# Two transformer layers with routed experts on one core: layer-norm chains of the attention moved to GpSimd and taken earlier, quantising moved off GpSimd, early shared sums added later

## What is computed

```python
x = x + quantised_product(layernorm(x), ctx)     # activations and ctx rounded to e4m3 in blocks of 128
x = x + moe(layernorm(x), 32 experts, top 4, plus a shared expert)
x = x + attention(layernorm(x), k=ctx, v=ctx)    # 8 heads of 32, 256 positions
x = x + moe(layernorm(x), 8 experts, top 2, plus a shared expert in two halves)
```

## Time and profile before

| | |
|---|---|
| median of 3 runs | 466.25 us (465.55 to 466.74) |
| the profiled execution | 468.48 us, of which the span of its instructions is 466.4 us |
| mean granted TensorE clock | 0.908 of full |
| busy share of the span | PE 76%, DVE 60%, ACT 43%, POOL 35% |

### The profile page before, as it was taken

One profiled execution on the slowest core, in us unless ns is written; L12 is line 12 of the kernel. 1 busy time (PEld: TensorE's weight loads), 2 busy tenths in 40 slices (PEclk: granted clock), 3 DMA queues, 4 the chain that ended last, 5 costly groups with the idle time before them and its releaser, 6 DMA issues.

```text
span 466.4 us, 8276 instructions
## 1 busy us (share of the span) xinstructions
PE 356.5 (76%) x2359; PEld 203.0 (44%) x2359; DVE 280.5 (60%) x791; ACT 201.7 (43%) x467; POOL 164.5 (35%) x220
## 2 busy tenths in 40 slices
PE   0003397789999999999983665667766899998996
PEld 0002184435555545555442444444554345444664
DVE  3999859645555555555558639395877155554365
ACT  1301245255555555555413737355731355554221
POOL 2060204756666666666310000002310533300560
PEclk9999998999999999999995558596985699999999
DMA  8999970094222322345557930000002223321232
GB/s 236 353 302 271 341 192 0 23 298 128 91 91 91 91 92 92 92 106 172 164 183 296 272 107 3 0 1 0 4 3 88 69 91 92 94 68 45 80 114 79
DMA packets 28780, 57.32 MB, mean 123 GB/s; under 512 B 3825, under 2 KB 13937, under 8 KB 28737
## 3 DMA queue, kind: packets, MB, share of 16 engines
q1 hardware_dynamic: 20785, 38.38, 27.0%
q0 software_dynamic: 6336, 17.31, 12.7%
q10 hardware_dynamic: 1616, 1.11, 0.8%
HBM read 44.72 MB, written 12.06 MB: 122 GB/s over the span
## 4 chain that ended last, share of the span: by engine, by line
PE 66%; DVE 18%; issue 8%; ACT 3%; POOL 2%; DMA 2%; DVEq 0%; ACTq 0%; SPq 0%; POOLq 0%
PE bank L1226 19%; PE bank L1253 13%; PE bank L1100 5%; PE bank L1237 5%; PE bank L1302 4%; PE bank L1217 3%; PE bank L1111 3%; PE bank L1314 3%; PE bank L1151 2%; PE bank L1089 2%; DMA x_sb<-x 2%; DVE x_sb L947 1%; DVE att_nm L979 1%; PE bank L1333 1%; DVE st L704 1%
## 5 line engine op out<-in xcount | busy, mean ns | idle before, releaser
L1226 PE MATMUL bank<-arena,xT 128*64 x272 | 112.5, 496 | 1.3 <-ACT xT L608 1.3
L1229 PE MATMUL bank<-xn,xT 128*64 128x384 f32 (+1 forms) x272 | 112.5, 497 | 0.0
L482 POOL DMA_INDIRECT xg<-m_xn,tab x68 | 65.7, 967 | 61.3 <-PE bank L1217 52.5
L1253 PE MATMUL bank<-arena,hT 96*64 (+1 forms) x272 | 70.4, 381 | 1.9 <-DVE hT L906 1.3
L1256 PE MATMUL bank<-xn,hT 96*64 96x256 f32 (+1 forms) x272 | 70.4, 381 | 0.0
L601 ACT ACTIVATE xn<-arena 128x768 f32 (+1 forms) x68 | 56.3, 827 | 21.9 <-issue 21.8
L931 DVE TENSOR_TENSOR hh<-sg,bank 128x192 f32<-128x192 f32 (+1 forms) x71 | 24.8, 350 | 63.0 <-ACT sg L624 63.0
L474 POOL DMA_INDIRECT m_ys<-ysb,dest x48 | 47.4, 988 | 23.9 <-issue 12.8
L1253 PEld LDWEIGHTS bank<-arena,hT 96*64 96x64 f32 (+1 forms) x272 | 34.8, 135 | 38.7 <-issue 28.2
L608 ACT ACTIVATE xT<-bank 128x256 f32<-128x256 f32 x71 | 27.2, 383 | 47.8 <-PE bank L1217 47.1
L1302 PE MATMUL bank<-arena,xn 32*128 32x256 f32 x128 | 23.0, 521 | 27.7 <-issue 21.4
(11 more groups left out here) (173 smaller groups left out, 615.2 us busy)
## 6 DMA issues: line engine op xcount, KB each, us to landing
arena<-w_gu SPq DMA_DIRECT2D x3, 3456.0 KB, 18.8
arena<-w_dn SPq DMA_DIRECT2D x3, 1728.0 KB, 24.5
arena<-m_ys SPq DMA_DIRECT2D x8, 512.0 KB, 5.5
m_ys<-ysb SPq DMA_DIRECT2D x20, 128.0 KB, 1.7
arena<-w_gu SPq DMA_DIRECT2D x2, 1056.0 KB
m_xn<-xn SPq DMA_DIRECT2D x2, 1024.0 KB, 6.4
arena<-w_gu SPq DMA_DIRECT2D x1, 1408.0 KB
arena<-w_gu SPq DMA_DIRECT2D x1, 1152.0 KB, 11.5
```

The source lines that it names most:

```text
L482: nc.gpsimd.indirect_dma_start(out=xg[:, b, :], out_offset=None, in_=xn_d[L.name], in_offset=bass.IndirectOffsetOnAxis(ap=d["tab"][:, s:s ...
L1226: T.matmul(bank[2 + s % 2][0:BLOCK, 0:2 * J2], xT[:, s % 2, c, 0:BLOCK], arena[:, bass.ds(off + c * 2 * J2, 2 * J2)], start=(c == 0), stop ...
L1229: return T.matmul(bank[2 + s % 2][BLOCK:P, 0:2 * J2], xT[:, s % 2, c, BLOCK:P], gu2[:, s % 2, cols], start=(c == 0), stop=(c == C - 1), ti ...
L1253: T.matmul(bank[6 + s % 2][0:BLOCK, 0:H], hT[0:L.J, s % 2, a, 0:BLOCK], arena[0:L.J, bass.ds(off + L.gu + a * H, H)], start=(a == 0), stop ...
```

## The change

- **Quantising.** The two GpSimd operations on ctx go to DVE: the addition right after the factors, the subtraction (to `wq`) between the two halves. The scaling of the normalised tokens leaves DVE for ACT, as 16 copies of 128 columns with a factor per token, in place; DVE waits for 8 of them before each half. The two three-operand forms on `amx` and `rin_x` become plain `tensor_scalar`. The semaphore `c_mag` is gone, `rin_ready` and `xs_ready` are new.
- **Early shared sums.** `early_shared` on GpSimd only multiplies. The additions to x stand in the loop of `gathers`, each ahead of the gather that waits for the same buffer's `t_done`. A result keeps its own buffer of `ysb` until then, so ACT no longer waits for the additions, and DVE no longer waits for all of them before the pair tiles; it waits for one of them before it writes that buffer.
- **Attention.** One table `chains` holds six chains: after which head the statistics are given, the tiles, whether they are for attention (then scaled, and normalised by ACT), and the head at which the result is used. GpSimd computes all six, with the negated means. Tiles 0 and 1 are one chain on DVE. Tiles 0 to 3 are taken before the first head, 4 to 7 at heads 1, 2, 6 and 7.

```diff
+        chains = [(-1, (2, 3), True, 2), (2, (4, 5), True, 7), (7, (6, 7), True, 12),
+                  (11, (0, 1), False, 15), (19, (2, 3), False, 23), (27, (4, 5), False, 31)]
...
-            pool.wait_ge(c_mag, 1)
-            link(nc.gpsimd.tensor_tensor(v_c, v_c, c_c, ALU.add))
-            nc.gpsimd.tensor_tensor(wq.rearrange("p b k n -> p (b k n)"), v_c, c_c, ALU.subtract).then_inc(wq_ready, 1)
...
+            def early_add(L, n):
+                q, t = M[L.name]["early"], early_work[L.name][n][1]
+                pool.wait_ge(q["y_copied"], n + 1)
+                nc.gpsimd.tensor_tensor(x_sb[:, t, :], x_sb[:, t, :], ysb[:, n, :], ALU.add).then_inc(q["added"], 1)
...
                     if s >= BUFS:
                         pool.wait_ge(m["t_done"], s - BUFS + 1)
+
+                        if s - BUFS < n_early[L.name]:
+                            early_add(L, s - BUFS)
...
             def deviations(i):
+                _, tiles, asked, _ = chains[i]
+                a, b = tiles[0], tiles[-1] + 1
                 pool.wait_ge(stats_ready, i + 2)
-                inverse_deviation(nc.gpsimd, link, by_pool[sorted(by_pool)[i]], 1.0)
-                pool.sem_inc(rstd_ready, 1)
+                inverse_deviation(nc.gpsimd, link, tiles, SCALE if asked else 1.0)
+                link(nc.gpsimd.tensor_tensor(nmr[:, a:b], mv[:, a:b, 0], rstd[:, a:b], ALU.mult))
+                nc.gpsimd.tensor_scalar(nmr[:, a:b], nmr[:, a:b], -1.0, None, ALU.mult).then_inc(rstd_ready, 1)
...
+            act.wait_ge(rin_ready, 1)
+            for a in range(16):
+                block_of = v_x[:, a * P:(a + 1) * P]
+                nc.scalar.activation(block_of, block_of, ACT.Copy, scale=rin_x[:, a:a + 1]).then_inc(xs_ready, 1)
...
-                if g in by_pair:
-                    queries(3 + sorted(by_pair).index(g), by_pair[g])
+                for i, (_, tiles_of, asked, turn) in enumerate(chains):
+                    if asked and turn == g:
+                        act.wait_ge(rstd_ready, i + 1)
+                        for t in tiles_of:
+                            normalise(t, q_ready)
...
-            link(V.scalar_tensor_tensor(out=amx[:], in0=amx[:], scalar=ACT_EPS, in1=amx[:], op0=ALU.max, op1=ALU.max))
+            link(V.tensor_scalar(amx[:], amx[:], ACT_EPS, None, ALU.max))
             link(V.reciprocal(rin_x[:], amx[:]))
-            link(V.scalar_tensor_tensor(out=rin_x[:], in0=rin_x[:], scalar=FP8_MAX, in1=rin_x[:], op0=ALU.mult, op1=ALU.max))
...
+            V.tensor_scalar(rin_x[:], rin_x[:], FP8_MAX, None, ALU.mult).then_inc(rin_ready, 1)
+
+            link(V.tensor_tensor(v_c, v_c, c_c, ALU.add))
...
+                dve.wait_ge(xs_ready, 8 * (i + 1))
...
+                if i == 0:
+                    V.tensor_tensor(wq.rearrange("p b k n -> p (b k n)"), v_c, c_c, ALU.subtract).then_inc(wq_ready, 1)
...
+            queries([0, 1])
+            take(2)
+            take(3)
+            statistics(chains[0][1]).then_inc(stats_ready, 1)
+            for g in range(4):
+                head_max(g)
+
+            takes = {1: 4, 2: 5, 6: 6, 7: 7}
```

More of the change, by code:

```diff
@@ L291, in mk_xattn_ffn @@
         n_early = {"m0": 4, "m1": 1}
+        assert max(n_early.values()) <= BUFS
         n_mid = {"m0": 1, "m1": 1}
@@ L507, in deviations @@
             def deviations(i):
+                _, tiles, asked, _ = chains[i]
+                a, b = tiles[0], tiles[-1] + 1
                 pool.wait_ge(stats_ready, i + 2)
-                inverse_deviation(nc.gpsimd, link, by_pool[sorted(by_pool)[i]], 1.0)
-                pool.sem_inc(rstd_ready, 1)
+                inverse_deviation(nc.gpsimd, link, tiles, SCALE if asked else 1.0)
+                link(nc.gpsimd.tensor_tensor(nmr[:, a:b], mv[:, a:b, 0], rstd[:, a:b], ALU.mult))
+                nc.gpsimd.tensor_scalar(nmr[:, a:b], nmr[:, a:b], -1.0, None, ALU.mult).then_inc(rstd_ready, 1)
             early_shared(L0)
             gathers(L0)
-            for i in range(len(by_pool)):
+            for i in range(len(chains)):
                 deviations(i)
@@ L574, in early_shared @@
                         act.wait_ge(q["d_done"], n)
-                        if n >= 3:
-                            act.wait_ge(q["added"], n - 2)
-                        nc.scalar.activation(ysb[:, (n - 1) % 2, :], bank[7][:, 0:H], ACT.Copy).then_inc(q["y_copied"], 1)
+                        nc.scalar.activation(ysb[:, n - 1, :], bank[7][:, 0:H], ACT.Copy).then_inc(q["y_copied"], 1)
             def after_shared(L, a, b):
@@ L655, in pT_copy @@
                                      ACT.Copy).then_inc(pT_ready, 1)
-            def queries(n, tiles):
-                act.wait_ge(chain_ready, n)
-                for t in tiles:
-                    normalise(t, q_ready)
-            queries(1, [0])
-            softmax_exp(0)
-            softmax_exp(1)
-            queries(2, [1])
-            softmax_exp(2)
+            act.wait_ge(chain_ready, 1)
+            for t in range(2):
+                normalise(t, q_ready)
+            for g in range(3):
+                softmax_exp(g)
             for g in range(nheads):
@@ L755, in _ @@
             link(V.tensor_reduce(amx[:], xn16, AX.X, ALU.max, apply_absolute_value=True))
-            link(V.scalar_tensor_tensor(out=amx[:], in0=amx[:], scalar=ACT_EPS, in1=amx[:], op0=ALU.max, op1=ALU.max))
+            link(V.tensor_scalar(amx[:], amx[:], ACT_EPS, None, ALU.max))
             link(V.reciprocal(rin_x[:], amx[:]))
-            link(V.scalar_tensor_tensor(out=rin_x[:], in0=rin_x[:], scalar=FP8_MAX, in1=rin_x[:], op0=ALU.mult, op1=ALU.max))
-            n = NT * H // 2
-            for i in range(2):
-                v16 = v_x[:, i * n:(i + 1) * n].rearrange("p (a n) -> p a n", n=P)
-                V.tensor_tensor(v16, v16, rin_x[:, 8 * i:8 * i + 8].unsqueeze(2).broadcast_to([P, 8, P]), ALU.mult)
+            V.tensor_scalar(rin_x[:], rin_x[:], FP8_MAX, None, ALU.mult).then_inc(rin_ready, 1)
+            link(V.tensor_tensor(v_c, v_c, c_c, ALU.add))
             for t in range(NT):
@@ L1019, in _ @@
                     take(takes[g])
-                if g in by_pair:
-                    queries(by_pair[g])
-                if g in by_pool:
-                    statistics(by_pool[g]).then_inc(stats_ready, 1)
-                if g - 3 in by_pool:
-                    dve.wait_ge(rstd_ready, sum(k <= g - 3 for k in by_pool))
-                    normalise(by_pool[g - 3], M["m1"]["xn_ready"])
+                for i, (given, tiles_of, asked, turn) in enumerate(chains):
+                    if given == g:
+                        statistics(tiles_of).then_inc(stats_ready, 1)
+                    if turn == g and not asked:
+                        dve.wait_ge(rstd_ready, i + 1)
+                        normalise(tiles_of, M["m1"]["xn_ready"])
                 if g + 4 < nheads:
```

39 lines of the change are left out of this document (13 added, 26 removed).

## The result

The changed kernel takes 453.42 us (median of 4 runs, 452.73 to 456.10) against 466.50 for the kernel before (median of 4) on the same chip: ratio 0.9725, 95% interval 0.9674 to 0.9776. It is 13 us faster. The prediction was 443.6 us, range 438 to 454: the direction is right and the time lies just inside the range, but the forecast gain was 22.7 us and 10 us of it did not come.

What follows compares the result with a forecast made beforehand. Attention was taken to wait for the query tiles' layer-norm chains, with quantising second: -4.0 + 0 - 17.8 - 0.9 = -22.7 from 468.48 gives 445.8; the median being 2.2 lower, 443.6 us, range 438 to 454.

Steps and rivals of the forecast that it cites:

- Quantising: DVE's quantising shortened, ACT's copies hidden: -4.0 us at the short end of copy times, -3.0 at the other.
- Early sums: Additions moved among the gathers on GpSimd: 0 us, between -0.7 and +2.9, because gathers run ahead.
- The worse end: Gather loop: all four additions ahead of gathers five to eight are felt, +2.9 us.
- The start of attention: Takes 0 to 3, one chain and statistics precede the first maximum, which comes 4.6 us later.
- Up to head 11: Attention walked at 1.2 GHz: late start paid back, maximum 11 ends at 282.1 against 282.55 before.
- Heads 11 to 31: Attention at 6.5 us per four heads: maximum 31 19.3 us earlier, 17.8 after 1.5 taken back for the clock.
- The clock rival: In attention the clock falls again or rises slowly, 4.1 us more per four-head group: 448 to 452 us, chance 0.25.
- The other rivals: Takes bound (0.10), late GpSimd chains (0.05), quantising not reaching the end (0.04), clock never rising (0.03), better 437 to 440 (0.08).
- the rival on the takes: Attention: the eight takes bound, pace nearer 2 than 1.6 us a head: 452 to 458 us, chance 0.10.
- The end: End of attention: statistics for the last chain 1.5 us earlier, chain 0.6 longer: -0.9 us.
- late chains: Attention: GpSimd's chains stretched, ACT waits up to 3 us at each of three turns: 447 to 452 us, chance 0.05.
- The signs: Profile checks, including ACT's wait for means under 10 us, no PE pause above 4 us, and full clock in attention.

Runs made afterwards that it cites:

- b_sums: Only the early shared sums' additions moved among the gathers, in the kernel before: 468.70 us, ratio 1.0014 to the kernel before.
- d_table: Changed kernel with statistics, normalising and takes 6 and 7 moved by one head, to stand behind the reciprocal: 447.06 us, ratio 0.9583 to the kernel before.
- k_nosums: Changed kernel with the early sums' additions back in their old place: 452.23 us, ratio 0.9663 to the kernel before.
- j_inv: `i_last` with the reciprocal issued ahead of maximum 4k+7: 444.66 us, ratio 0.9482 to the kernel before.
- i_last: `d_table` with the last pair's normalising put behind the layer norm of tile 6: 445.67 us, ratio 0.9527 to the kernel before.
- f_both: `d_table` with the reciprocal issued first and the tile's result behind maximum 4k+7: 447.33 us, ratio 0.9566 to the kernel before.
- g_start: `f_both` with takes 2 and 3 put ahead of maxima 2 and 3, tiles 2 and 3 normalised at head 3: 449.28 us, ratio 0.9613.
- l_best: `j_inv` with the early sums' additions in their old place: 444.67 us, ratio 0.9495 to the kernel before.

## Why the prediction was right and wrong

**Quantising, -4.0: right.** 4.28 in the trace and 4.2 alone on the clock. ACT's eight copies took 2.4 us, a little below the short end, and were hidden. The rule of the Trainium skill ("ScalarE: Activation LUTs", What ACT_TABLE_LOAD costs) gave an estimated 2.4 for them, and the trace agrees: 0.30 us a copy.

**Early sums, 0 between -0.7 and +2.9: not refuted.** Alone they measure +0.7, between -0.3 and +1.6. "PE reaches the token table at nearly the same time" is confirmed by `b_sums`, where the freed POOL waits 4.0 us and the gather starts at the same moment. The worse end, four additions in line ahead of the gathers, is what the trace shows at 90 to 98 us; of the delay 0.3 and 0.8 us are left at the eighth and ninth gather.

**The start of attention, +4.6: right.** The first maximum stands 12.59 us behind take 0, before 7.98.

**Up to head 11, about level: right but 1 us short.** Maximum 11 starts 38.87 us behind take 0; the working has it at 281.45, which is 37.84 behind take 0 of before. The walk at 1.2 GHz was right up to 272; from there to 276 the clock read 0.78.

**Heads 11 to 31: wrong, the term that was mis-sized.** The step was "Five groups of four are 32.5; ACT's normalising of tiles 6 and 7 adds 1.0", with 1.5 taken back for the clock: 35.0 us. Measured: 40.2. With the 1.0 of the stretch before it, this is, but for 0.1, the whole of 17.8 less 11.5. The 6.5 us of the earlier trace rows were no property of the heads but of a ring, and in the rows between 303.30 and 309.81 the take stood behind the reciprocal, outside it. "Even with a take among them" was therefore read wrongly: it showed that a take is free in that place, not that it is free anywhere. The working counted DVE's work in sum ("nothing but maxima, results and a few statistics is left") and did not ask which of it PE's `values` wait for. `d_table` shows it: with the same work moved by one head the five groups from maximum 10 to 30 take 34.5 us instead of 42.3, three of them the 6.5 of the forecast. Maximum 11 to 31 is 34.5 us. That this is so near the forecast's 33.5 + 1.5 is in part luck: `d_table` had the full clock throughout, so that the 1.5 held for the clock was not needed, and the group with ACT's normalising cost 1.6 more than the others instead of 1.0.

**The clock rival, chance 0.25, 448 to 452: in part right, but as a consequence.** The working of this rival names "a take and statistics between heads 10 and 11, and PE may stand 2 to 4 us". So it was:

```profile
278.00:279.00 1.00, 0.00 (x0) 0.00 (x0) 0.93 (x3) 0.31 (x1) 0.00 (x0) 1.00 0.00 0
...
280.00:281.00 1.00, 0.00 (x1) 0.01 (x1) 0.99 (x5) 0.13 (x1) 0.49 (x3) 0.77 0.00 0
281.00:282.00 1.00, 1.00 (x20) 0.93 (x24) 1.00 (x2) 1.00 (x5) 0.69 (x4) 0.50 0.00 0
```

These are windows of the changed kernel: stretch, its length, busy PE, PEld, DVE, ACT and POOL with their counts, granted clock, DMA share, GB/s. PE stood some 4 us for the reciprocal behind take 7 and the statistics, the clock fell to the 1.2 GHz level, and `values` was done at it. This is the longest pause, over the 4 us that the prediction had named as a sign of being wrong:

```profile
281.00 1.08 PE L1330 MATMUL bank<-ident,arena 128*32 128x128 f32 x16 [4.24 <-DVE arena L992]
```

What the clock cost is the smaller part: by the estimate above 2.5 of the 7.8 us that `d_table` won back in these groups, where the forecast had held 1.5 for it. Ahead of the second fall, at 297.6, there is no such pause: PE's pauses ahead of it were 1.47, 0.40, 0.52 and 0.77 us, and in `k_nosums` it came a group later. The other rivals did not come. ACT waited once only for the means, so GpSimd's chains were in time at heads 2, 7 and 12. What running beside a take cost them stands in the last two operations of the chain of tiles 4 and 5 on POOL, which fell beside the take at 270.09:

```profile
270.13 0.49 POOL L513 TENSOR_TENSOR nmr<-mv,rstd 128x2 f32<-128x2 f32 x1
270.71 0.46 POOL L514 TENSOR_SCALAR nmr<-nmr 128x2 f32<-128x2 f32 x1
```

They took 0.49 and 0.46 us, where the same two of the first chain took 0.19 and 0.24: 0.5 us in all, against 5 us of cover. The pace of 2 us a head that the rival on the takes had came about (40.2 us for 20 heads), but by the place of the work and the clock, not by the takes' sum.

**The end, -0.9: right.** From maximum 31 to the end of the span 132.1 became 130.6, -1.5, and DVE's wait for the last chain is gone.

**The sum.** In the two traces the terms are -2.3 up to take 0, -11.5 and -1.5, together -15.3; the medians show -13.1, because the changed kernel's profiled execution was the fastest of its four and the one of before lay 2 us above its median. That 453.42 is still inside the range is luck: the upper end of 454 was there for the clock, for late chains and for the takes, and no rival names the reciprocal.

**The signs.** Those on quantising, on the first maximum and on ACT's wait came as written. Two others did not: PE paused for 4.24 us, and slices 23 and 24, in attention, still read 5. The second contradicts the prediction's own working, which walks this stretch at 1.2 GHz.

## What to carry to other kernels

When a pace is read off a quick stretch, find the ring that makes it, operation by operation, and see on which side of its hand-over each other instruction stands. Here work moved off a wait cost its whole duration where it landed between the two ends of such a ring, as long as no other wait ended later, and nothing one instruction further on. On an in-order engine, issue what another engine waits for (here a reciprocal of 0.19 us) ahead of everything that merely has to be done, and never behind a wait for a third engine.

## What was not expected of the hardware

The granted clock fell in one kernel and not in another after nearly the same pauses. In `d_table` and in `j_inv` PE stood twice, for 1.60 and 0.77 us in the one and 1.64 and 0.77 in the other, waiting for ACT's copies. Windows of `d_table`, then of `j_inv` (columns as above):

```profile
283.00:284.00 1.00, 0.80 (x6) 0.67 (x8) 1.00 (x4) 1.00 (x6) 0.72 (x4) 1.00 0.00 0
284.00:285.00 1.00, 1.00 (x16) 0.62 (x18) 0.40 (x4) 1.00 (x4) 0.51 (x4) 1.00 0.00 0
```
```profile
283.00:284.00 1.00, 0.23 (x3) 0.03 (x1) 0.97 (x3) 1.00 (x4) 0.76 (x4) 0.67 0.00 0
284.00:285.00 1.00, 1.00 (x4) 0.69 (x4) 0.96 (x4) 1.00 (x5) 0.66 (x4) 0.50 0.00 0
```

In the second `scores`, the turns and `values` went at 1.2 GHz for some 7 us and the group took 10.7 us where the other took 8.1. Ahead of these pauses each had one short pause, of 0.37 us in `j_inv` and 0.54 in `d_table`, and the clock of `j_inv` had risen later, 1.4 us ahead of maximum 10, that of `d_table` 2.5. `i_last`, with the attention order of `d_table` up to head 30, had it rise 2.5 us ahead and kept it as well; `f_both`, `g_start` and `l_best`, with the reciprocal first, had it rise 1.1 to 1.7 us ahead and lost it in the same group, which took 10.8, 10.6 and 10.6 us. Whether the order of the work or the moment of the rise decides it no run here shows.
